# Small operands as weights in four groups of array columns: the heads' score products of a four-layer graph network

## The chip, the cores and the metric

The kernel runs on one core of a Trainium2 chip. The metric is the device time of one execution in microseconds (us), the median of several runs.

## What is computed

Four graph layers over 3327 nodes with 128 features each; after each layer comes x = layernorm(x + layer(x)). The adjacency matrix `adj` (3327 x 3327, float32) is the same in all. The change touches layer 4, whose attention part is, cut down:

```python
def _gat_head(h, node_adj, edge_adj, W, a):        # 3 heads, ALPHA = 0.2
    hW = h @ W
    hp = (node_adj > 0).astype(hW.dtype) @ hW
    hm = (node_adj < 0).astype(hW.dtype) @ hW
    e_plus = leaky_relu(concatenate([hp, hm], axis=1) @ a, ALPHA)[:, 0]
    e_minus = leaky_relu(concatenate([hm, hp], axis=1) @ a, ALPHA)[:, 0]
    att = where(edge_adj > 0, e_plus[None, :], NEG_INF)
    att = where(edge_adj < 0, e_minus[None, :], att)
    return softmax(att, axis=1) * edge_adj @ hW
...
node_support = node_adj_norm @ h                   # adj without its diagonal
edge_output = _gru_cell(node_support, h, edge_Wih, edge_Whh, edge_bih, edge_bhh)
edge_support = mean over the heads of _gat_head(h, node_adj_norm, edge_adj_norm, gat_W[i], gat_a[i])
node_output = _gru_cell(edge_support, h, node_Wih, ...)
return de[:, None] * edge_output + dn[:, None] * node_output
```

Since `(A > 0) @ (h @ W) @ a` is `(A > 0) @ (h @ (W a))`, the kernel needs only, for each node, six numbers `h @ (W a)` (two halves of `a` for three heads: the **column scores**), and the pattern sums of these. Of the sums, three a node are the heads' **raw scores**, from which e_plus follows.

## The kernel before, in words

Nodes are padded to 3328 and stand in 26 tiles of 128 (`TILES`); the columns of the adjacency in 7 blocks (`BLOCKS`, six of 512 and one of 256; `NB` = 7, `BT` = 4 tiles a block). SBUF tiles of note: `x` (nodes on partitions), `xT` (its transpose, features on partitions), `ring` (13 slots of 128 x 512 for pieces of `adj`), `pos8` (the pattern adj > 0 in fp8, in `arena`), `V` (in `shared`, the pattern sums), `es`/`unb` (scratch, in `es`), `hb`. `ps` is PSUM, 8 banks of 128 x 512 float32.

Layer 4's first half is one queue on TensorE, written out by hand:

- `dense4(b, between)` multiplies block b of adj with x: 26 products of 512 columns (L1169) into bank b % 2, each waiting for its slot of the ring; `between` names what is done behind which tile. SyncE refills a slot when its product has freed it (L493), so loads run 13 tiles ahead. GpSimd zeroes the diagonal piece of four tiles a block (`ring_cuts`, L639) before they are used (`cut_ring`).
- `turn` (L973) transposes x into xT, with ScalarE's `turn_copy` (L685) emptying banks 2 and 3.
- Column scores (L1178): for each of the 26 tiles, 128 columns of xT are the weights and the six columns of `v6` the moving operand; results go to bank 3. VectorE splits them into three bf16 parts in `gs` (L1744 to L1749, from PSUM directly).
- `edge_gates(g)` (L1149 to L1151) are the products of the gated cell for two tiles, four of them in blocks 1 and 2, whose element work VectorE (`edge_cell`, L1760 to L1781) and ScalarE (L808, L812) do.
- `pattern_sums` (L1190): V = gs-columns x pos8, on strips of 32 array columns, t % 4 choosing the strip; ScalarE copies each block of V out of PSUM (L826). SyncE writes V to DRAM once it is complete (`kept`, L507), between the ring's loads of tiles 12 and 13 of block 2.
- Raw scores (L1206): for each of 26 tiles, 128 columns of V are the weights and three columns of `selE` (0 and 1, adding up the 32-row strips) the moving operand; results go to bank 2. VectorE (L1818 on) takes leaky relu, the heads' maxima (`turn_maxima`, L1211), a rounded maximum spread to all partitions (`spread_maxima`, L1215), the range (`turn_range`, L1219), and the window weights `wh` (to L1862).
- `window_sums` (L1231) with `turn_sums` (L1239) stand behind block 3; the head loop (L1321) ends the first half's work.

The column scores stand between `turn` and block 1, the raw scores between the pattern sums and block 2:

```python
                pe.wait_ge(xT_done, 2 * NB)
                for t in range(TILES):
                    last = mm(ps[:, 3, 6 * t:6 * t + 6], lhsT=xT[:, t * P:(t + 1) * P],
                              rhs=v6[:].rearrange("p a k -> p (a k)"), start=True, stop=True)
```

Of the kernel before, what the change touches and what calls it, by code (L numbers as in the profile page):

```python
# [38 lines left out]
def program(nc, d, out):  # L39
    ctx = ExitStack()  # L40
    with ctx:
# [3 lines left out]
        def sem(name):  # L45
            return ctx.enter_context(nc.semaphore(name))
# [11 lines left out]
        def piece(space, at, width):  # L58
            return space[:, at:at + width]
# [39 lines left out]
        gscr = piece(bench, 0, 6 * TILES).rearrange("p (t r) -> p t r", r=6)  # L99
# [24 lines left out]
        v6 = sb("v6", [P, 2, HEADS])  # L124
# [94 lines left out]
        cols_done = sem("cols_done")  # L219

# [199 lines left out]
        def tiles_of(b):  # L420
            return range(b * BT, min((b + 1) * BT, TILES))

# [239 lines left out]
        def _(act):  # L662
# [156 lines left out]
            for b in range(NB):  # L819
                turn_copy(NB + b, b, 2 + b % 2)  # L820
            edge_cell(0)
            edge_cell(1)
            u3_copy(1)
            for b, (o_, w) in enumerate(BLOCKS):
                act.wait_ge(v_done, b + 1)
                A_(V[:, o_:o_ + w], ps[:, 2 + b % 2, 0:w], ACT.Copy).then_inc(v_out, 1)  # L826
            act.wait_ge(est, TT_READY)
# [117 lines left out]
        def _(pe):  # L945
# [146 lines left out]
            def after_layer2(negative):  # L1092
# [82 lines left out]
                turn(2 * TILES, NB, (2, 3))  # L1175
                pe.wait_ge(xT_done, 2 * NB)
                for t in range(TILES):
                    last = mm(ps[:, 3, 6 * t:6 * t + 6], lhsT=xT[:, t * P:(t + 1) * P],  # L1178
                              rhs=v6[:].rearrange("p a k -> p (a k)"), start=True, stop=True)
                last.then_inc(cols_done, 1)  # L1180
                dense4(1, {4: lambda: edge_gates(0), 14: lambda: edge_gates(1)})
# [22 lines left out]
                pe.wait_ge(v_out, NB)  # L1204
                for t in range(TILES):
                    last = mm(ps[:, 2, HEADS * t:HEADS * (t + 1)], lhsT=V[:, t * P:(t + 1) * P], rhs=selE[:, 0:HEADS], start=True, stop=True)  # L1206
                last.then_inc(raw_done, 1)
# [13 lines left out]
                dense4(2, {2: turn_maxima, 4: spread_maxima, 8: turn_range, 12: lambda: edge_gates(2), 20: lambda: edge_gates(3)})  # L1221
# [146 lines left out]
        def _(ve):  # L1368
# [23 lines left out]
            def late_steps():  # L1392
                ve.wait_ge(late_prod, 1)
                step(v.tensor_copy(v6[:], ps[:, 6, 0:2 * HEADS].rearrange("p (k a) -> p a k", a=2)))
                step(v.tensor_tensor(gru[:, 3], gru[:, 3], ps[:, 6, P:P + G3], ALU.subtract))
                check(steps[0], V6_READY)
                step(v.tensor_tensor(b2[:], b2_two[:, 0], b2_two[:, 1], ALU.add))
                check(steps[0], B2_READY)
                step(v.tensor_tensor(gb[:, :, 1:3].rearrange("p e a f -> p e (a f)"),
                                     gb[:, :, 1:3].rearrange("p e a f -> p e (a f)"), stage, ALU.add))  # L1400
                step(v.scalar_tensor_tensor(state_weights[:, 0:G3], state_weights[:, 0:G3], lone[:], gru[:, 3], ALU.mult, ALU.add))
                step(v.tensor_scalar(state_weights[:, G3:], state_weights[:, G3:], lone[:], None, ALU.mult))
                step(v.tensor_scalar(others[:], lone[:], -1.0, 1.0, ALU.mult, ALU.add))
                step(v.tensor_copy(ident16, ident[:]))
                check(steps[0], LATE_READY)

# [335 lines left out]
            g6 = ps[:, 3, 0:6 * TILES].rearrange("p (t r) -> p t r", r=6)  # L1742
# [75 lines left out]
            then(v.tensor_copy(raw, ps[:, 2, 0:Q78]))  # L1818
# [267 lines left out]
V6_READY = 35  # L2086
B2_READY = 36
LATE_READY = 41
GS_READY = 53
# [5 lines left out]
OUT_READY = 57  # L2095
# [48 lines left out]
```

## Time and profile before

| | us |
|---|---|
| three runs: median (lowest to highest) | 1450.9 (1450.29 to 1452.09) |
| profiled execution: span from first to last instruction (the one time it gives) | 1449.1 |
| its TensorE matmuls busy | 1339.7 (92%) |
| VectorE busy | 906.9 (63%) |
| ScalarE busy | 543.8 (38%) |
| GpSimd busy | 187.7 (13%) |
| mean granted TensorE clock | 0.966 of full |

The page of a profile is one execution. PE is TensorE's matmuls, PEld its weight loads, DVE VectorE, ACT ScalarE, POOL GpSimd, SPq the queue of SyncE's DMAs. The span leaves out what lies before the first and behind the last instruction: the runs' median is 1.8 above it. A float32 product stands in the trace as two matmul records, so "x52" at L1178 is 26 products. Layer 4's first half runs from 668 us to about 927 us.

### The profile page before, as it was taken

To read this page: it belongs to the slowest core of one execution; us is meant where nothing else is said; L and a number is where in the kernel's file an instruction comes from. 1 tells how busy PE (TensorE), PEld (TensorE's weight loads), DVE (VectorE), ACT (ScalarE), POOL (GpSimd) and SP (SyncE) were. 2 spreads that over 40 slices of the span, in tenths; PEclk is the share of its full clock that TensorE was granted. 3 is DMA by queue.
4 is the path that set the end of the run, shared out by engine and by line. 5 is a ranking of instruction groups with operands and counts; after the bars stand their busy time and mean duration, and the time that the engine had idled before them with its cause. 6 is when DMAs were issued, how large, how long until landed. Compare 5 with 4: busy or idle time off the path is not lost.

```text
span 1449.1 us, 11441 instructions
## 1 busy us (share of the span) xinstructions
PE 1339.7 (92%) x4198; PEld 675.7 (47%) x4198; DVE 906.9 (63%) x1187; ACT 543.8 (38%) x469; POOL 187.7 (13%) x211
## 2 busy tenths in 40 slices
PE   3888886899989999999999999999999999999993
PEld 1333334444444444455655454644445444544451
DVE  4787777888865000003125363599878987898576
ACT  4444444867630000000111001455564565555333
POOL 0000002000020000000000000124431244113111
PEclk9999997899999999999899999999999999999997
DMA  9999993000026767758447339698876888688301
GB/s 380 427 426 416 419 390 107 2 0 0 0 96 175 196 192 196 193 150 275 149 164 236 105 109 325 211 363 327 307 281 252 329 304 310 229 306 329 141 0 50
DMA packets 78002, 321.27 MB, mean 222 GB/s; under 512 B 8685, under 2 KB 20588, under 8 KB 61036
## 3 DMA queue, kind: packets, MB, share of 16 engines
q1 hardware_dynamic: 77931, 320.40, 61.9%
q8 instruction: 37, 0.61, 0.2%
q14 instruction: 34, 0.27, 0.1%
HBM read 316.94 MB, written 3.43 MB: 221 GB/s over the span
## 4 chain that ended last, share of the span: by engine, by line
PE 82%; DMA 10%; DVE 5%; ACT 1%; issue 1%; SPq 0%; POOL 0%; ACTq 0%; DVEq 0%; POOLq 0%
PE ps L1321 29%; PE ps L1132 10%; PE ps L1169 10%; PE ps L1066 10%; DMA ring<-in_adjR 9%; PE ps L991 6%; PE ps L1126 5%; PE ps L1231 2%; PE ps L1342 1%; PE ps L1303 1%; PE ps L1150 1%; PE ps L1343 1%; DMA ring<-in_adjB 1%; PE ps L1106 1%; PE ps L1151 1%; PE ps L1190 1%
## 5 line engine op out<-in xcount | busy, mean ns | idle before, releaser
L1321 PE MATMUL ps<-arena,x 128*128 128x512 f32 (+1 forms) x1092 | 438.9, 562 | 2.9 <-ACT shared L894 1.6
L1321 PEld LDWEIGHTS ps<-arena,x 128*128 128x128 f32 x1092 | 206.1, 190 | 231.4 <-issue 225.2
L887 ACT ACTIVATE arena<-arena,bench 128x3328 f32<-128x3328 bf16 x78 | 239.8, 3075 | 188.8 <-PE ps L1321 176.4
L991 PE MATMUL ps<-ring,bench 128*128 128x512 f32 (+1 forms) x364 | 171.9, 617 | 51.1 <-DMA ring<-in_adjR 48.9
L1982 DVE TENSOR_TENSOR arena<-arena,ring 128x3328 f32<-128x3328 f32 x51 | 184.9, 3625 | 27.3 <-ACT arena L887 26.8
L1132 PE MATMUL ps<-ring,x 128*128 128x512 f32 (+1 forms) x364 | 176.2, 566 | 0.0
L1169 PE MATMUL ps<-ring,x 128*128 128x512 f32 (+1 forms) x364 | 152.1, 573 | 1.0 <-DMA ring<-in_adjB 1.0
L991 PEld LDWEIGHTS ps<-ring,bench 128*128 128x128 f32 x364 | 70.8, 206 | 130.6 <-issue 97.1
L1691 DVE SCALAR_TENSOR_TENSOR bench<-b,cols,ps 128x128 f32<-128x128 f32 x26 | 7.3, 343 | 183.1 <-PE ps L1106 183.1
L651 POOL TENSOR_TENSOR ring<-ring,nid 128x128 f32<-128x128 f32 x51 | 86.0, 1686 | 205.2 <-DMA ring<-in_adjR 205.2
L1126 PE MATMUL ps<-arena,shared 128*128 128x512 fp8e4 (+1 forms) x364 | 103.6, 366 | 6.1 <-DVE shared L1496 6.1
L1982 DVE TENSOR_TENSOR arena<-arena 128x3328 f32<-128x3328 f32 x27 | 98.1, 3632 | 13.0 <-ACT arena L887 13.0
L1169 PEld LDWEIGHTS ps<-ring,x 128*128 128x128 f32 x364 | 69.9, 194 | 72.6 <-issue 67.8
L1066 PE MATMUL ps<-ring,x 128*128 128x512 f32 (+1 forms) x196 | 82.2, 576 | 6.0 <-DVE ring L1616 5.7
L795 ACT ACTIVATE ub<-ps 128x512 f32<-128x512 f32 (+1 forms) x7 | 4.0, 567 | 208.2 <-PE ps L1132 208.2
L1126 PEld LDWEIGHTS ps<-arena,shared 128*128 128x128 f16 x364 | 35.7, 98 | 96.7 <-issue 85.5
L1132 PEld LDWEIGHTS ps<-ring,x 128*128 128x128 f32 x364 | 67.7, 192 | 23.1 <-issue 0.5
L1975 DVE TENSOR_SCALAR arena<-arena,bench 128x3328 bf16<-128x3328 bf16 x52 | 62.2, 1195 | 0.0
L1066 PEld LDWEIGHTS ps<-ring,x 128*128 128x128 f32 x196 | 37.4, 194 | 50.2 <-issue 47.6
L651 POOL TENSOR_TENSOR arena<-arena,nid 128x128 f32<-128x128 f32 x27 | 46.0, 1707 | 105.7 <-DMA arena<-in_adjR 105.6
L1440 DVE TENSOR_SCALAR arena<-ring 128x3328 fp8e4<-128x3328 f32 x26 | 49.0, 1883 | 1.2 <-DMA ring<-in_adjR 1.2
L1760 DVE TENSOR_TENSOR es<-ps,gb 128x512 f32<-128x512 f32 x12 | 8.3, 691 | 61.7 <-PE ps L1151 61.7
(289 smaller groups left out, 1427.8 us busy)
## 6 DMA issues: line engine op xcount, KB each, us to landing
ring<-in_adjR SPq DMA_DIRECT2D x77, 1664.0 KB, 8.7
ring<-in_adjB SPq DMA_DIRECT2D x312, 256.0 KB, 3.1
arena<-in_adjR SPq DMA_DIRECT2D x27, 1664.0 KB, 8.4
shared<-in_adj SPq DMA_DIRECT2D x7, 1664.0 KB, 13.4
es<-in_adj SPq DMA_DIRECT2D x7, 1664.0 KB, 13.4
xT<-in_adj SPq DMA_DIRECT2D x6, 1664.0 KB, 13.0
y<-in_adj SPq DMA_DIRECT2D x6, 1664.0 KB, 13.4
ring<-in_adjB SPq DMA_DIRECT2D x52, 128.0 KB, 2.3
```

What stands on the lines that cost most here:

```text
L651: g_.tensor_tensor(cut, cut, nid[:], ALU.mult).then_inc(row_cut, 1)
L887: A_(E[n % 3], below[n % 3], ACT.Exp, bias=tt_[:, t * HEADS + k:t * HEADS + k + 1], scale=-WIN).then_inc(e_exp, 1)
L991: op = mm(ps[:, b, 0:w], lhsT=scaled[:, t % 4], rhs=turned_tile[t % 2][:, o_:o_ + w], start=(t == 0), stop=(t == TILES - 1))
L1066: op = mm(ps[:, b, 0:w], lhsT=x[:, t], rhs=EL[t % 4][:, o_:o_ + w], start=(t == 0), stop=(t == TILES - 1))
L1126: mm(ps[:, 2 + par, 0:w], lhsT=x16[:, t, k], rhs=pos8[:, t, o_:o_ + w], start=first and k == 0, stop=final and k == 1)
L1132: mm(ps[:, par, 0:w], lhsT=x[:, t], rhs=ring[:, t % CHUNKS, 0:w], start=first, stop=final).then_inc(ring_free, 1)
L1169: mm(ps[:, b % 2, 0:w], lhsT=x[:, t], rhs=ring[:, t % CHUNKS, 0:w], start=(t == 0), stop=(t == TILES - 1)).then_inc(ring_free, 1)
L1231: last = mm(ps[:, b % 2, 0:w], lhsT=wh[:, t], rhs=pos8[:, t, o_:o_ + w], start=(t == 0), stop=(t == TILES - 1))
L1321: last = mm(ps[:, b, 0:w], lhsT=x[:, t], rhs=E[n % 3][:, o_:o_ + w], start=(t == 0), stop=(t == TILES - 1))
L1440: v.tensor_scalar(pos8[:, t], turned_tile[t % 2], 0.0, None, ALU.is_gt, saturate=False).then_inc(pos_done, 1)
L1975: v.tensor_scalar(below[n % 3], tops[k], raw[:, t * HEADS + k:t * HEADS + k + 1], 0.0, ALU.add, ALU.max).then_inc(lowered, 1)
L1982: v.tensor_tensor(E[n % 3], E[n % 3], row_at(n), ALU.mult).then_inc(q_ready, 1)
```

## The change

Both score groups swap their operands. The small operand (`v6`, now 32 columns wide with zeroes, or `some`, a copy of selE's three columns, also padded to 32) becomes the weights and a whole block of xT or V, 512 columns, moves. Block b's product goes to the array columns 32 (b % 4) and the partitions of the same numbers, in bank 2 for blocks 0 to 3 and bank 3 for blocks 4 to 6: seven products in place of 26 (`strips`). The scores now stand with nodes along the free axis, so ScalarE copies both banks to SBUF (`rows_copy`, in the scratch `unb`), and eight transposes (`turn_strips`) put nodes back on partitions. VectorE gathers the scores from PSUM by `by_tile`, three copies a group. The transposes, and for the raw scores the strips too, stand between products of blocks 1 and 2. In block 2 the later steps move: maxima behind tile 6 (2), spread 8 (4), range 12 (8), gates 14 and 21 (12 and 20).

```diff
-        v6 = sb("v6", [P, 2, HEADS])
+        padded = hb[:, 1, 0:64]
+        v6 = padded[:, 0:32]
+        some = padded[:, 32:64]
+        scores = unb
...
+        def by_tile(bank, rows):
+            by = ps[:, bank, :].rearrange("p (s q r) -> p q s r", s=BT, q=4)
+            if bank == 2:
+                return [(slice(0, 4 * BT), by[:, :, :, 0:rows])]
+            return [(slice(4 * BT, 6 * BT), by[:, 0:2, :, 0:rows]), (slice(6 * BT, TILES), by[:, 2, 0:TILES - 6 * BT, 0:rows])]
...
+            def rows_copy(done, out_):
+                act.wait_ge(done, 1)
+                A_(scores[:, 0], ps[:, 2, :], ACT.Copy).then_inc(out_, 1)
+                A_(scores[0:96, 1], ps[0:96, 3, :], ACT.Copy).then_inc(out_, 1)
+
+            rows_copy(scored, scores_out)
             edge_cell(0)
...
                 A_(V[:, o_:o_ + w], ps[:, 2 + b % 2, 0:w], ACT.Copy).then_inc(v_out, 1)
+            rows_copy(picked, picked_out)
...
+                def strips(weights, rows, done):
+                    for b, (o_, w) in enumerate(BLOCKS):
+                        q = 32 * (b % 4)
+                        last = mm(ps[q:q + 32, 2 + b // 4, 0:w], lhsT=weights, rhs=rows[:, o_:o_ + w], start=True, stop=True)
+                    last.then_inc(done, 1)
+
+                def turn_strips(out_, done):
+                    pe.wait_ge(out_, 2)
+                    for h, k in ((0, P), (1, 96)):
+                        for s in range(BT):
+                            last = nc.tensor.transpose(ps[:, 2 + h, s * P:s * P + k], scores[0:k, h, s * P:(s + 1) * P], ident[0:k, 0:k])
+                    last.then_inc(done, 1)
+
                 pe.wait_ge(xT_done, 2 * NB)
-                for t in range(TILES):
-                    last = mm(ps[:, 3, 6 * t:6 * t + 6], lhsT=xT[:, t * P:(t + 1) * P],
-                              rhs=v6[:].rearrange("p a k -> p (a k)"), start=True, stop=True)
-                last.then_inc(cols_done, 1)
-                dense4(1, {4: lambda: edge_gates(0), 14: lambda: edge_gates(1)})
+                strips(v6, xT, scored)
+                dense4(1, {2: lambda: turn_strips(scores_out, cols_done), 4: lambda: edge_gates(0), 14: lambda: edge_gates(1)})
...
-                pe.wait_ge(v_out, NB)
-                for t in range(TILES):
-                    last = mm(ps[:, 2, HEADS * t:HEADS * (t + 1)], lhsT=V[:, t * P:(t + 1) * P], rhs=selE[:, 0:HEADS], start=True, stop=True)
-                last.then_inc(raw_done, 1)
+                def pick():
+                    pe.wait_ge(v_out, NB)
+                    strips(some, V, picked)
...
-                dense4(2, {2: turn_maxima, 4: spread_maxima, 8: turn_range, 12: lambda: edge_gates(2), 20: lambda: edge_gates(3)})
+                dense4(2, {1: pick, 3: lambda: turn_strips(picked_out, raw_done), 6: turn_maxima, 8: spread_maxima, 12: turn_range,
+                           14: lambda: edge_gates(2), 21: lambda: edge_gates(3)})
...
-                step(v.tensor_copy(v6[:], ps[:, 6, 0:2 * HEADS].rearrange("p (k a) -> p a k", a=2)))
+                step(v.memset(padded, 0.0))
+                v.tensor_copy(some[:, 0:HEADS], selE[:, 0:HEADS])
+                step(v.tensor_copy(v6[:, 0:2 * HEADS].rearrange("p (a k) -> p a k", a=2), ps[:, 6, 0:2 * HEADS].rearrange("p (k a) -> p a k", a=2)))
...
-            g6 = ps[:, 3, 0:6 * TILES].rearrange("p (t r) -> p t r", r=6)
+            for bank in (2, 3):
+                for ts, got in by_tile(bank, 6):
+                    of = g6[:, ts] if len(got.shape) == 3 else g6[:, ts].rearrange("p (q s) r -> p q s r", s=BT)
+                    op = v.tensor_copy(of, got)
+            step(op)
...
-            then(v.tensor_copy(raw, ps[:, 2, 0:Q78]))
+            for bank in (2, 3):
+                for ts, got in by_tile(bank, HEADS):
+                    of = raw[:, ts.start * HEADS:ts.stop * HEADS]
+                    op = v.tensor_copy(of.rearrange("p (t k) -> p t k", k=HEADS) if len(got.shape) == 3
+                                       else of.rearrange("p (q s k) -> p q s k", s=BT, k=HEADS), got)
+            then(op)
```

TensorE's queue from the column scores into block 1, before (the lines are the kernel's; a row is a run of equal instructions, output <- operands, shape of the output; `v` is v6):

```order
L1178 MATMUL ps<-v,xT 128x6 x26
L1169 MATMUL ps<-ring,x 128x512 x5
L1149 MATMUL ps<-gru,ub 128x128
L1150 MATMUL ps<-gru,xT 128x384
L1151 MATMUL ps<-gru,ub 128x256
```

and with the change, where line numbers have moved (L1199 the strips, L1206 the turns back, L1189 the dense products, L1169 to L1171 the gates; `hb` holds v6, `es` the copied rows):

```order
L1199 MATMUL ps<-xT,hb 32x512 x6
L1199 MATMUL ps<-xT,hb 32x256
L1189 MATMUL ps<-ring,x 128x512 x3
L1206 MATMUL ps<-ident,es 128x128 x4
L1206 MATMUL ps<-ident,es 128x96 x4
L1189 MATMUL ps<-ring,x 128x512 x2
L1169 MATMUL ps<-gru,ub 128x128
L1170 MATMUL ps<-gru,xT 128x384
L1171 MATMUL ps<-gru,ub 128x256
```

26 products before block 1 have become seven, and eight transposes stand behind block 1's third tile.

TensorE's queue from the raw scores through block 2's first steps, before:

```order
L1206 MATMUL ps<-selE,shared 128x3 x26
L1169 MATMUL ps<-ring,x 128x512 x3
L1211 MATMUL ps<-ident,mx 3x128
L1169 MATMUL ps<-ring,x 128x512 x2
L1215 MATMUL ps<-dm,ones 128x3
L1169 MATMUL ps<-ring,x 128x512 x4
L1219 MATMUL ps<-ident,rmax 1x128
```

and with the change:

```order
L1199 MATMUL ps<-shared,hb 32x512 x6
L1199 MATMUL ps<-shared,hb 32x256
L1189 MATMUL ps<-ring,x 128x512 x2
L1206 MATMUL ps<-ident,es 128x128 x4
L1206 MATMUL ps<-ident,es 128x96 x4
L1189 MATMUL ps<-ring,x 128x512 x3
L1240 MATMUL ps<-ident,mx 3x128
L1189 MATMUL ps<-ring,x 128x512 x2
L1244 MATMUL ps<-dm,ones 128x3
L1189 MATMUL ps<-ring,x 128x512 x4
L1248 MATMUL ps<-ident,rmax 1x128
L1189 MATMUL ps<-ring,x 128x512 x2
```

Block 2's first two tiles now follow the pattern sums directly; strips, two tiles, the turns back, and three more tiles come before the maxima's transpose (L1240), then spread (L1244) and range (L1248) at the old distances.

## Rows read from the trace of the kernel before

**Rows 1.** Page, part 4: the chain that ended last, by engine.

```profile
PE 82%; DMA 10%; DVE 5%; ACT 1%; issue 1%; SPq 0%; POOL 0%; ACTq 0%; DVEq 0%; POOLq 0%
```

**Rows 2.** Chain from 665 to 940 us: start us, us, what ran, matmul records.

```profile
668.07 22.33 PE ps L1169 x52
...
695.35 9.49 PE ps L1178 x52
704.84 5.81 PE ps L1169 x10
...
733.88 9.96 PE ps L1190 x175
...
743.86 0.39 ACT shared L826
...
744.29 7.42 PE ps L1206 x52
751.71 4.55 PE ps L1169 x6
...
821.62 0.44 PE ps L1239 x4
822.05 5.61 PE ps L1231 x26
```

**Rows 3.** Busy time by window: stretch, us, busy per engine (count), granted clock (PEclk).

```profile
core 0: us, PE busy (x) PEld busy (x) DVE busy (x) ACT busy (x) POOL busy (x), PEclk, DMA share, GB/s
...
690.40:695.30 4.90, 3.51 (x26) 2.50 (x24) 0.00 (x0) 4.13 (x8) 0.00 (x0) 1.00 0.54 184
695.30:697.30 2.00, 1.95 (x18) 1.95 (x18) 0.00 (x0) 1.28 (x1) 0.00 (x0) 1.00 0.00 0
697.30:704.80 7.50, 7.50 (x38) 7.50 (x37) 0.00 (x0) 0.00 (x0) 0.00 (x0) 0.50 0.01 2
704.80:707.60 2.80, 2.80 (x5) 1.25 (x5) 2.04 (x6) 0.00 (x0) 0.00 (x0) 0.51 0.00 0
...
744.20:748.50 4.30, 4.21 (x38) 4.21 (x38) 0.00 (x0) 0.04 (x1) 0.00 (x0) 1.00 0.82 346
748.50:751.70 3.20, 3.20 (x17) 3.20 (x16) 0.00 (x0) 0.00 (x0) 0.00 (x0) 0.51 0.18 73
751.70:755.20 3.50, 3.50 (x6) 1.43 (x6) 0.74 (x3) 0.00 (x0) 0.00 (x0) 0.50 0.07 12
```

**Rows 4.** Line L1190 alone: ns min/median/max of a record, shapes, counts.

```profile
L1190 PE MATMUL ps<-arena,gs x182: 272/379/393, 733.8 to 743.5; 128*32 128x512 fp8e4 x156, 128*32 128x256 fp8e4 x26
```

**Rows 5.** Timeline of ScalarE, 742 to 762 us: start, us, line, [idle before].

```profile
743.09 0.60 ACT L826 ACTIVATE shared<-ps 128x512 f32<-128x512 f32 x1 [0.91 <-PE ps L1190]
```

**Rows 6.** Timeline of VectorE, 690 to 850 us, same columns.

```profile
704.88 0.48 DVE L1744 CAST gs<-ps 128x156 bf16<-128x156 f32 x1 [33.22 <-PE ps L1178]
...
751.75 0.24 DVE L1818 COPY bench<-ps 128x78 f32<-128x78 f32 x1 [22.45 <-PE ps L1206]
...
752.30 0.26 DVE L1820 TENSOR_REDUCE mx<-bench 128x3 f32<-128x78 f32 x1
756.48 0.28 DVE L1823 TENSOR_REDUCE mq<-ps 3x1 f32<-3x128 f32 x1 [3.93 <-PE ps L1211]
...
757.32 0.22 DVE L1827 TENSOR_SCALAR dm<-ident,mq 3x3 f32<-3x3 f32 x1
...
762.25 0.28 DVE L1842 TENSOR_REDUCE row<-ps 1x1 f32<-1x128 f32 x1 [1.70 <-PE ps L1219]
...
771.44 0.20 DVE L1862 TENSOR_SCALAR bench<-bench 128x78 f32<-128x78 f32 x1
```

**Rows 7.** DMA issues, 735 to 765 us: count, KB each, us to landing.

```profile
ring<-in_adjB SPq DMA_DIRECT2D x12, 256.0 KB, 3.1
V_kept<-shared SPq DMA_DIRECT2D x1, 1664.0 KB, 6.1
```

**Rows 8.** Timeline of TensorE, 860 to 945 us, same columns.

```profile
927.08 5.75 PE L1321 MATMUL ps<-arena,x 128*128 128x512 f32 x14
```

More of the change, by code:

```diff
@@ L98, in program @@
         raw, e_, dd, idx, ctr, tt_, r1, r2, v_ = (piece(bench, k * Q78, Q78) for k in range(9))
-        gscr = piece(bench, 0, 6 * TILES).rearrange("p (t r) -> p t r", r=6)
+        gscr, g6 = (piece(bench, k * 6 * TILES, 6 * TILES).rearrange("p (t r) -> p t r", r=6) for k in range(2))
         hb = sb("hb", [P, 2, F])
@@ L219, in program @@
         cols_done = sem("cols_done")
+        scored = sem("scored")
+        scores_out = sem("scores_out")
+        picked = sem("picked")
+        picked_out = sem("picked_out")
         f1_done = sem("f1_done")
@@ L2085 @@
 XSB_READY = 27
[L2086 to L2089, printed above, removed]
+V6_READY = 36
+B2_READY = 37
+LATE_READY = 42
+GS_READY = 55
 MX_READY = 3
@@ L2094 @@
 WH_READY = 23
-OUT_READY = 57
+OUT_READY = 59
 DOWN = 2.718281828459045 ** -64
```

## The prediction, made before the changed kernel had run

> **What bounds the kernel now.** I read the chain that ended last first, then the chain inside layer 4's first half, then the granted clock along it, and last the timelines of the engines that TensorE hands over to. The page's chain is 82% TensorE [rows 1], so work taken off TensorE counts unless something else was about to end at the same time. In the stretch that the change touches the chain is all TensorE [rows 2]: block 0's 26 tiles (52 records, two passes each, since every float32 product here leaves two matmul records) take 22.33 us, that is 0.859 us a tile; then come the turns of x, the column scores at L1178 (9.49 us), block 1, the pattern sums at L1190 (9.96 us), a wait for ScalarE's last copy of V (from 733.88 + 9.96 = 743.84 to 744.29, 0.45 us), the raw scores at L1206 (7.42 us), and block 2.
>
> The reader is to see three things. First, the two score groups are bound by weights, not by columns: 26 products of 6 columns cost 0.365 us each and 26 of 3 columns 0.285 us each, with the weight loads busy for all of the stretch (1.95 of 2.00 us, 7.50 of 7.50) [rows 3]. Second, the clock: while x is turned it is granted in full, two microseconds into the column scores it falls to half (1.2 GHz instead of 2.4) and stays there until 707.6, well into block 1; in the raw scores it falls at 748.5 and is back only at 755.2 [rows 3]. So block 1's first 5 tiles took 5.81 us where 5 x 0.859 = 4.29 are usual, and block 2's first 3 took 4.55 instead of 2.58 [rows 2]. Third, nothing but the two groups' consumers hangs on them: VectorE waits 33 us for the column scores and 22 us for the raw ones [rows 6].
>
> **The change, part by part.** Removed from the chain: L1178 9.49, L1206 7.42, the 0.45 ahead of it (two tiles of block 2 now stand there instead, 1.7 us), and the half-clock tails 5.81 - 4.29 = 1.52 and 4.55 - 2.58 = 1.97. Sum 20.85 us. The tails go only if the clock holds, which is a rival below.
>
> Added, for each group: seven products with 32 columns of weights, six of 512 moving columns and one of 256. What such a product costs in float32 is not in the trace, so I bound it. One after the other they take as much as dense tiles, 6 x 0.859 + 0.43 = 5.58 us. Four at once, as the pattern sums do it, they take two rounds, 2 x 0.859 = 1.72. That strips on 32 columns do run side by side is shown: L1190's 182 products (156 of 512 columns, 26 of 256, so 169 full ones) last 9.96 us, 0.059 each [rows 2, 4], against 0.216 for a one-pass product on all columns (5.61 us for 26) [rows 2]. But there neighbours in the queue are always different strips. Here each product is two passes on the **same** strip, in order: the second pass of strip 0 waits for the first, and only strip 1's first pass can run beside it. Then a pass starts every 0.43 us and the group takes 6 x 0.43 + 0.43 = 3.0 us. I take 3.0, between the ends 1.7 and 5.6, since queues of matmuls start in order in every row I have.
>
> The Trainium skill (TensorEngine Tiling (Array Packing), Theoretical Speedup) gives up to four times for a dimension of 32 or less, and says nothing there of two passes. By it the group would take the 1.72 us of the last end and the sum below would be 2.6 us larger; that is the first rival.
>
> Around a group the array goes from all columns to strips and back. L1190 shows the most this can cost: 9.96 us against 169 x 0.216 / 4 = 9.13, so 0.83 with seven hand-overs to ScalarE in it. I take 0.3 a group, ends 0 and 0.8.
>
> The eight turns back: four turns take 0.44 us between products [rows 2], so eight take 0.88, and the four of 96 columns no more. Per group 3.0 + 0.3 + 0.88 = 4.2 us, both 8.4. **Sum: 20.85 - 8.4 = 12.45, say 12.5 us off TensorE's chain.**
>
> What stands beside other work, with its cover. ScalarE copies the two banks: 0.60 us each [rows 5], with hand-overs some 1.4 us from the last strip to the turns' start. The cover is three dense tiles (2.58 us) in block 1 and two (1.72 us) in block 2; the second has 0.3 us to spare, and without cover the cost is at most 1.4 us each. ScalarE is idle at both places. VectorE takes three small copies in place of one (0.24 us for the raw ones [rows 6], 0.5 more), three for the column scores where there were none (up to 0.48 each, 1.4 us), and a memset and a copy far earlier in layer 3. The column scores' chain, 704.88 to 707.1, is wanted only by L1190 a block later. The raw scores' chain: 752.56 - 751.75 = 0.8 us to the heads' maxima, now 1.3, behind three dense tiles (2.58). From the maxima to the spread two tiles, 1.72 us, against the five steps from 756.48 to 757.54, 1.06 us and a hand-over on either side [rows 6]; from there to the range four tiles as before, where VectorE even waited 1.70 us [rows 6]. The chain to the window weights ends 9.4 us behind the range turn (762.25 to 771.64) [rows 6]. Block 2's gates now come at 14 and 21 instead of 12 and 20, still behind it or level; the next taker, the window sums, is over 30 us away.
>
> SyncE and GpSimd: no DMA is moved in the order. The load of block 2's tile 13 stands behind the write of V, 6.1 us [rows 7], which waits for V's last copy. It used to run beside L1206; now it runs beside block 2's own tiles. The ring holds 13 tiles, 11 us of products, plus strips and turns, so tile 13's load has about 15 us for 6.1 + 3. After that the ring has to refill at the pace of the products: 26 loads of 256 KB in 22.33 us without a wait, as in block 0 [rows 2, 7]. I cost it at nothing; if the lead were gone it would be a few tenths a tile.
>
> Everything behind block 2 starts from TensorE's own progress (frees of the ring, window sums, head loads), so the 12.5 us should reach the end whole. Span 1449.1 - 12.5 = 1436.6; the runs' median 1450.9 lies 1.8 above the span, so the forecast is **1438.4 us**.
>
> **The rivals.** *Four at once.* For: L1190 does it. Against: two passes on one strip. Groups of 1.72 instead of 3.0: 1435.8 us.
>
> *One at a time.* If a two-pass product holds the whole array, or strips with different moving data can't overlap in this type: 5.58 a group, 5.2 us less gain, 1443.6 us. For it speaks only that no two-pass strip is in the trace.
>
> *The clock falls anyway.* Here a stretch of half clock lasts 10.3 and 6.7 us [rows 3], and costs half of that in work: 5.1 + 3.4 = 8.5 us, so 1446.9. For: x's turns come right before, with TensorE busy only 3.5 of 4.9 us [rows 3], and the strips are short. Against: the clock was 1.00 through the turns and fell only in the 6-column products [rows 3], and through L1190's strips the chain ran at full pace. The Trainium skill (TensorE: Matmul & The Clock Gate, Part 4: PE-mode transpose) says that turns don't count as activity, which would make this case likelier; the trace here disagrees as far as it goes, since five microseconds of turns left the clock at 1.00.
>
> *Slower.* The strips run one after the other **and** at half clock throughout, at L1178's place and at block 2's: 2 x 5.58 + 2 x 0.88 + 0.3 = 13.2 us a group, and the tails of 3.5 us stay. 26.4 + 3.5 against 20.9 is 9.0 us longer, 1459.9. It decides from 10.4 us a group; one of the two halves alone doesn't reach it.
>
> *It moves nothing.* The ring or VectorE gives the gain back (a wait in block 2 of the size of the gain), about 1450. The rows show leads of 15 us and over 30 us against it.
>
> **How the numbers follow.** Pairs 0.45, four at once 0.25, one at a time 0.16, clock falls 0.08, moves nothing 0.03, slower 0.03. The predicted time is that of pairs. The range goes from four at once with no cost of switching (1435.8 less 0.6, and a half more for a clock that shifts elsewhere) to one at a time with the dear switching (1443.6 + 1.0): 1434.6 to 1444.8. Left out are the clock case and the last two. A measurement of this kernel tells some 0.2%, 2.9 us, from no change. All cases but the last two are faster by more: 0.94; within 0.03; slower 0.03.
>
> **What would show it.** In the new profile the strips' line shows 14 records a group in about 3 us, their starts 0.43 us apart: 0.86 apart would be one at a time, groups of starts together four at once. The granted clock from 695 to 715 and around 745 reads 1.00, and block 1's first tiles take 0.86. TensorE waits for neither ScalarE's copies nor the ring in blocks 1 and 2. The head loop's first matmul starts about 12.5 us before 927.08 [rows 8]. A group above 5 us, a clock of 0.50 behind it, or a shift that shrinks before 927 would each prove a step wrong.

## The result

The changed kernel takes 1434.53 us (median of four runs, 1432.49 to 1435.09) against 1450.81 before (four runs too): ratio 0.9882, 95% interval 0.9866 to 0.9898, so 16 us or 1.2% faster. The forecast was 1438.4 with a range from 1434.6 to 1444.8. The direction held, the size didn't: the gain is 4 us larger, and the time lies just below the range, by 0.07 us, which is less than the runs differ among themselves.

The profiled execution's span is 1433.5 us instead of 1449.1. Its chain, in the page's part 4:

```profile
PE 83%; DMA 9%; DVE 5%; ACT 1%; issue 1%; SPq 0%; POOL 0%; ACTq 0%; DVEq 0%; POOLq 0%
```

And the chain through layer 4's first half (start us, us, what; the rows answer to [rows 2]):

```profile
668.57 22.33 PE ps L1189 x52
...
695.85 1.91 PE ps L1199 x12
697.76 2.77 PE ps L1189 x6
700.53 0.77 PE ps L1206 x8
701.30 1.75 PE ps L1189 x4
...
726.27 9.94 PE ps L1220 x176
736.21 1.91 PE ps L1189 x4
738.12 1.84 PE ps L1199 x12
739.96 1.91 PE ps L1189 x4
741.88 0.77 PE ps L1206 x8
742.64 2.60 PE ps L1189 x6
...
795.78 11.38 PE ps L1261 x52
```

Block 0 takes the same 22.33 us. The column scores' 9.49 us have become 1.91, the raw scores' 7.42 us 1.84, the turns back 0.77 each. Block 1's first three tiles take 2.77 us, where before its first five took 5.81. From block 0's first tile to the first window sum the stage takes 795.78 - 668.57 = 127.21 us; before it took 810.23 - 668.07 = 142.16 (its last row below, with the end of the next stretch). So 14.95 us went here, of 15.6 in the whole span.

```profile
810.23 11.38 PE ps L1231 x52
...
936.29 3.64 DVE arena L1982
```

The head loop's first matmul starts at 911.35 instead of 927.08 [rows 8], 15.7 us earlier. The granted clock is now full all through the stage (answering to [rows 3]; stretch, us, busy us and count per engine, granted clock, DMA share, GB/s):

```profile
690.90:695.80 4.90, 3.50 (x26) 2.50 (x24) 0.00 (x0) 4.14 (x8) 0.00 (x0) 1.00 0.46 153
695.80:697.80 2.00, 1.95 (x15) 0.52 (x16) 0.00 (x0) 0.00 (x0) 0.00 (x0) 1.00 0.00 0
697.80:703.00 5.20, 5.20 (x20) 2.76 (x21) 1.53 (x7) 2.36 (x3) 0.00 (x0) 1.00 0.55 150
...
738.10:740.00 1.90, 1.90 (x16) 0.46 (x16) 0.00 (x0) 0.00 (x0) 0.00 (x0) 1.00 0.88 364
740.00:745.30 5.30, 5.30 (x20) 2.75 (x21) 0.87 (x5) 1.08 (x2) 0.00 (x0) 1.00 0.66 231
```

The rest of the 15.6: from the window sums to the head loop's second row 124.79 us instead of 126.06, 1.27 less; the head of the program, up to block 0, 0.50 more; the head loop and all behind it 0.12 more. The 1.27 goes with the wait for a load of the ring in block 5, 1.01 us before and absent in this profile. It isn't something the change aims at. In the profiles below the wait is 2.0 us (e5), 1.2 (e2), 0.9 (e4), 0.7 (e3), 0.6 (e7), 0.5 (e8) and absent (e1, e6, e9, e10). The other 0.26 comes and goes with it: less their wait, all seven profiles that have it take 125.05 to 125.07 us for this stretch, while this profile, e1 and e9 take 124.79 to 124.88 (e6, without a wait that shows, takes 125.18).

How four strips share the array is seen best in the strips' own line, in steps of 0.05 us through the raw scores' group (busy us and records of TensorE's products, then of its weight loads):

```profile
738.05:738.10 0.05, 0.05 (x4) 0.05 (x8) 1.00 2.50 1065
738.30:738.35 0.05, 0.05 (x4) 0.00 (x0) 1.00 0.00 0
738.50:738.55 0.05, 0.05 (x8) 0.04 (x3) 1.00 1.94 799
738.75:738.80 0.05, 0.05 (x4) 0.00 (x0) 1.00 0.00 0
738.90:738.95 0.05, 0.05 (x7) 0.01 (x3) 1.00 0.00 0
739.35:739.40 0.05, 0.05 (x5) 0.00 (x0) 1.00 0.00 0
739.60:739.65 0.05, 0.05 (x2) 0.00 (x0) 1.00 2.51 1065
```

Four products start together at 738.05, and all eight weight loads of the four strips' first products, for both passes, are under way within those 0.05 us. Until 738.5 there are four records, then eight overlap for a moment (the second passes start, the ends of the first are modelled), four again, and at 738.9 the next round's first three, which are the passes of blocks 4 to 6. No pass of strip 1 waited for the second pass of strip 0.

### The profile page after: what moved, and what is told of

Its sections match the earlier page's. It is cut to its first block, busy times and chain, and to the rows that moved or that the text cites. A ratio compares the mean times of both kernels' runs of the same rounds, so it can differ in the third digit from the quotient of the medians.

```text
span 1433.5 us, 11332 instructions
## 1 busy us (share of the span) xinstructions
PE 1322.4 (92%) x4138; PEld 658.3 (46%) x4138; DVE 906.7 (63%) x1194; ACT 546.0 (38%) x473; POOL 189.3 (13%) x211
## 4 chain that ended last, share of the span: by engine, by line
PE 83%; DMA 9%; DVE 5%; ACT 1%; issue 1%; SPq 0%; POOL 0%; ACTq 0%; DVEq 0%; POOLq 0%
PE ps L1351 30%; PE ps L1152 10%; PE ps L1189 10%; PE ps L1086 10%; DMA ring<-in_adjR 8%; PE ps L1011 6%; PE ps L1146 5%; PE ps L1261 2%; PE ps L1372 1%; PE ps L1333 1%; PE ps L1170 1%; PE ps L1373 1%; PE ps L1126 1%; DMA y<-in_adj 1%; PE ps L1171 1%; PE ps L1220 1%
## 5 line engine op out<-in xcount | busy, mean ns | idle before, releaser
L1189 PE MATMUL ps<-ring,x 128*128 128x512 f32 (+1 forms) x364 | 149.2, 563 | 0.0
L1189 PEld LDWEIGHTS ps<-ring,x 128*128 128x128 f32 x364 | 68.3, 190 | 69.8 <-issue 67.4
L1657 DVE TENSOR_TENSOR ring<-ring,arena 128x3328 f32<-128x3328 f32 x13 | 46.8, 3617 | 0.0
```

The lines of the kernel that those rows point to most:

```text
L1189: mm(ps[:, b % 2, 0:w], lhsT=x[:, t], rhs=ring[:, t % CHUNKS, 0:w], start=(t == 0), stop=(t == TILES - 1)).then_inc(ring_free, 1)
L1657: v.tensor_tensor(EL[t % 4], EL[t % 4], pos8[:, t], ALU.mult).then_inc(q1, 1)
```

## The experiments

Since the head of the program alone moves by up to 6 us from one execution to the next (block 0's first tile starts between 666.4 and 672.3 us in the twelve profiles), single spans can't tell 2 us. I compare the stage from block 0's first tile to the first window sum, which is 142.16 us before and 127.21 changed (127.23 in a second profile, e9).

**e1: neighbours in the queue on the same strip.** Blocks 0 and 1 go to the same strip, in banks 2 and 3, blocks 2 and 3 to the next, and so on. ScalarE's copies keep their shape; VectorE's copies follow the new layout.

```diff
-                        q = 32 * (b % 4)
-                        last = mm(ps[q:q + 32, 2 + b // 4, 0:w], lhsT=weights, rhs=rows[:, o_:o_ + w], start=True, stop=True)
+                        q = 32 * (b // 2)
+                        last = mm(ps[q:q + 32, 2 + b % 2, 0:w], lhsT=weights, rhs=rows[:, o_:o_ + w], start=True, stop=True)
```

> The strips' products stand in the other order: blocks 0 and 1 are neighbours in the queue and go to the same strip of 32 array columns (one in bank 2, one in bank 3), blocks 2 and 3 to the next, and so on; the amount of work and all that follows is the same. In the changed kernel a group takes 1.84 us between the tiles around it. Theory A (each strip has its own order; a product that waits for its strip doesn't hold up those behind it for other strips): a group stays at 1.7 to 2.0 us, four matmul records start together at its beginning, and the kernel's time stays at that of the changed kernel within 1 us. Rival B (matmuls start in the order of the queue, and the changed kernel ran four at once only because neighbours were on different strips): strip 0's four passes run first and the next strip joins only at its last one, 4 to 4.5 us a group, some 5 us longer in all.

The chain of e1, same columns:

```profile
699.57 1.93 PE ps L1199 x11
701.51 2.77 PE ps L1189 x6
...
741.87 1.86 PE ps L1199 x11
```

and the strips' line at the start of its first group, as above for the changed kernel:

```profile
699.60:699.65 0.05, 0.05 (x4) 0.05 (x8) 1.00 0.00 0
```

1.93 and 1.86 us, and the stage 127.26: theory A. With two products a strip, what stands next to what in the queue doesn't matter: a product whose strip is busy doesn't hold up those behind it. Four records are under way 0.05 us into the group (a strip works on one at a time, as e7 shows below), so the fourth strip's product runs although six stand ahead of it, of which three, one a strip, still wait. That is the step of my prediction that fails (e1's time, 1438.9 us, is no counter-argument: block 0 starts at 672.29 here, 3.7 us late before anything changed has run).

**e7: one strip with more work than the others.**

```diff
-                    for b, (o_, w) in enumerate(BLOCKS):
+                    for b, (o_, w) in [(0, BLOCKS[0])] * 3 + list(enumerate(BLOCKS)):
```

> The changed kernel with block 0's product issued four times instead of once in each group (same weights, same result, three idle repeats), so that strip 0 has five products, and the other strips two, two and one. Theory A (each strip works off its own products; a group takes as long as its longest strip): 5 x 0.859 = 4.3 us a group, 2.4 more than the 1.84 to 1.91 now. Rival B (the work is shared over the strips, ten products in rounds of four): three rounds, 2.6 us a group. Rival C (in order of the queue, pairs): strip 0's four products first and the rest behind, 5.2 us or more.

```profile
697.78 4.48 PE ps L1199 x18
702.26 2.77 PE ps L1189 x6
...
742.63 4.41 PE ps L1199 x18
```

4.48 and 4.41 us a group, where five products of two passes one behind the other are 5 x 0.859 = 4.3. Rival B's 2.6 and rival C's 5.2 are both excluded. The stage is 132.36, 5.15 above the changed kernel. So a group's time here is that of its fullest strip: with the seven blocks spread over four strips, two products, 1.72, plus 0.12 to 0.19.

That time alone doesn't show that the strips are free of each other, and the weight loads of this group show that they are not quite (timeline of TensorE's weight loads in e7, 697 to 703 us, columns as in [rows 6]):

```profile
697.78 0.14 PEld L1199 LDWEIGHTS ps<-xT,hb 128*32 128x32 f32 x2 [0.71 <-ACT xT L698]
698.24 0.11 PEld L1199 LDWEIGHTS ps<-xT,hb 128*32 128x32 f32 x1 [0.32 <-issue]
...
699.10 0.11 PEld L1199 LDWEIGHTS ps<-xT,hb 128*32 128x32 f32 x1 [0.32 <-issue]
699.53 0.15 PEld L1199 LDWEIGHTS ps<-xT,hb 128*32 128x32 f32 x7 [0.32 <-issue]
```

For the first 1.7 us only strip 0 works, one pass after the other, and the other three strips stand empty although their products are in the queue; the second group does the same (742.60 to 744.30). They start when the third of the four products at the head of the queue starts and only the fourth still waits. So in these runs one waiting product a strip is passed over (e1 has one on each of three strips), and two on the same strip hold up all that stands behind them. It costs nothing here only because strip 0 is the fullest either way.

**e5 and e6: one group alone.** e5 swaps the column scores only, e6 the raw scores only; the other group's lines are those of the kernel before.

```diff
# e5
-            rows_copy(picked, picked_out)
...
-                def pick():
-                    pe.wait_ge(v_out, NB)
-                    strips(some, V, picked)
+                pe.wait_ge(v_out, NB)
+                for t in range(TILES):
+                    last = mm(ps[:, 2, HEADS * t:HEADS * (t + 1)], lhsT=V[:, t * P:(t + 1) * P], rhs=selE[:, 0:HEADS], start=True, stop=True)
+                last.then_inc(raw_done, 1)
# e6
-            rows_copy(scored, scores_out)
...
-                strips(v6, xT, scored)
-                dense4(1, {2: lambda: turn_strips(scores_out, cols_done), 4: lambda: edge_gates(0), 14: lambda: edge_gates(1)})
+                for t in range(TILES):
+                    last = mm(ps[:, 3, 6 * t:6 * t + 6], lhsT=xT[:, t * P:(t + 1) * P], rhs=v6[:, 0:6], start=True, stop=True)
+                last.then_inc(cols_done, 1)
+                dense4(1, {4: lambda: edge_gates(0), 14: lambda: edge_gates(1)})
```

> Only the column scores are swapped, the raw scores stand as in the kernel before. Measured from block 0's first tile to the first window sum, where the kernel before takes 142.16 us and the changed one 127.21. Theory (the two groups are independent terms, each with its clock tail): L1178's 9.49 and the tail of 1.52 go, 1.84 for the strips and 0.77 for the turns and about 0.2 around them come: 142.2 - 8.2 = 134.0 us. The granted clock is 1.00 from 690 to 735 and falls once, in the raw scores. Rival (the second group only keeps its clock because the first no longer lowers it): the raw scores' stretch shows no fall here, and this kernel takes under 133.

> Only the raw scores are swapped, the column scores stand as in the kernel before. Theory (independent terms): L1206's 7.42, the wait of 0.45 and the tail of 1.97 go, 1.84 + 0.77 and about 0.4 around them come: 142.2 - 6.8 = 135.4 us from block 0 to the window sums, with the clock at 0.50 once, in the column scores and in block 1's first tiles. Both parts together are then 15.0, the whole of the change. Rival: a part that only the two together give, seen as a sum of both savings below 13.

e6 takes 135.33 us, 6.8 less than before, as expected. e5 takes 135.68, 6.5 less instead of 8.2. Its chain shows why:

```profile
736.59 9.21 PE ps L1235 x52
745.80 4.39 PE ps L1188 x6
```

The raw scores, the same 26 products as before, take 9.21 us here instead of 7.42: the clock fell 2.3 us into them, at 738.9, not 4.2 us in as in [rows 3], and was back at 749.1:

```profile
738.50:739.00 0.50, 0.50 (x6) 0.50 (x6) 0.00 (x0) 0.00 (x0) 0.00 (x0) 0.88 0.91 373
```

Nothing in these lines changed, only when they ran. So the two savings add up to 13.3, and the missing 1.6 of 14.95 is the clock's: what a stretch of small products costs hangs on when the clock happens to fall in it. The rival of e5 (no fall, under 133) is wrong, and so is my figure, and with it the 15.0 that I expected of the two parts together; e6's rival, a sum below 13, isn't met either.

The same rows give the price of a small product at each clock. At full clock 38 records, 19 products, take 4.21 us [rows 3], 0.22 us each. Counted at that price at full clock and at twice that price at half clock, 26 of them come to 9.5, 7.3 and 9.2 us for the column scores before, the raw ones before and the raw ones in e5 (2.0, 4.2 and 2.3 us of them at full clock), against 9.49, 7.42 and 9.21 measured. The 0.365 and 0.285 us of the prediction are mixtures of the two.

**e2 and e8: the old products, but never alone.** No operands swapped. The 26 small products a group stand between dense tiles: in e2 two behind each of 13 tiles in blocks 1 and 2; in e8 block 2 has four behind each of its first seven, so that VectorE gets the raw scores earlier. The other steps of block 2 move back, and VectorE splits the column scores between the two gated cells of block 1.

```diff
+                def some_cols(n):
+                    for t in (2 * n, 2 * n + 1):
+                        last = mm(ps[:, 3, 6 * t:6 * t + 6], lhsT=xT[:, t * P:(t + 1) * P],
+                                  rhs=v6[:].rearrange("p a k -> p (a k)"), start=True, stop=True)
+                    if n == TILES // 2 - 1:
+                        last.then_inc(cols_done, 1)
...
+                steps2 = {t + 1: (lambda n=t: some_raw(n)) for t in range(13)}
+                steps2.update({15: turn_maxima, 17: spread_maxima, 21: turn_range, 23: lambda: edge_gates(2), 25: lambda: edge_gates(3)})
# e8
+                steps2 = {t + 1: (lambda n=t: some_raw(n)) for t in range(7)}
+                steps2.update({9: turn_maxima, 11: spread_maxima, 15: turn_range, 17: lambda: edge_gates(2), 23: lambda: edge_gates(3)})
```

> The kernel before, with its 26 small products a group unchanged (128 columns of weights, 6 or 3 moving columns), but spread: two of them behind each of 13 dense tiles in block 1 and in block 2, so that the engine never runs a stretch of small products alone. The maxima, the spread and the range come at tiles 15, 17 and 21, the gates of block 2 at 23 and 25. Theory (the clock falls because of the stretch of small products, and the two tails of 3.5 us are part of what the change gains): granted clock 1.00 from 668 us to the window sums, block 1's and 2's tiles at 0.86 each, and each small product 0.285 us or less, as at full clock before: 9.49 + 7.42 become 14.8 or less, tails and the wait of 0.45 gone, so 6 us faster than before, near 1444.8; up to 10 us faster if a part of the weight loads hides behind the dense passes (0.2 a product). Rival 1 (the clock falls on its own, after the turns): still 0.50 for some 7 to 10 us in each block, and at most 1 us faster. Rival 2 (the swap brings nothing of its own, keeping the groups apart does it all): as fast as the changed kernel, 1434.5.

> As e2, the old small products between dense tiles, but the raw ones four behind each of block 2's first seven tiles instead of two behind thirteen, with the maxima, spread and range at tiles 9, 11 and 15 and the gates at 17 and 23. In e2 the clock held, a small product cost 0.22 us (0.34 a pair and 0.10 on the tile behind it), and the gain was given back in block 3, where TensorE waited 5.4 us for ScalarE's copy because VectorE was late with the window weights. Theory: that chain is 5 to 6 us earlier and the wait goes; the clock stays at 1.00; the stage from block 0 to the window sums takes 142.2 - 9.4 = 132.8 us, 5.6 longer than with strips. Rival (four small products between tiles lower the clock, or the chain is still late): over 135.

The 0.285 us that e2's text gives as the price at full clock is such a mixture; the price was 0.22.

e2: ratio to before 0.9981 (0.9966 to 0.9995), the stage 140.65 us, only 1.5 less where 6 were expected. But the parts went as the theory says. Block 1's steps (one tile, two small products) and what came of it in block 3, in the chain:

```profile
698.21 0.34 PE ps L1179 x4
698.55 0.96 PE ps L1169 x2
...
742.53 0.34 PE ps L1217 x4
...
783.97 0.59 ACT ub L804
...
784.60 0.80 PE ps L1149 x2
```

and TensorE's waits from 665 to 930 us (engine, line, what for: us in total, times, longest):

```profile
PE ps L1149 <- ACT ub L804: 5.9, 2, 5.4
PE ps L1169 <- DMA ring<-in_adjB: 1.2, 1, 1.2
```

Two small products take 0.34 us and the tile behind them 0.10 more, so 0.22 each, the same as alone at full clock: standing between large products doesn't make a small one cheaper, it keeps the clock. The granted clock is 1.00 from 668 to 784 us. A group's small products cost 5.7 us, with no tail. What it gave was then lost in block 3: the raw scores were ready 13 tiles late, VectorE's chain to the window weights ended behind them, the gated cells queued up behind it, ScalarE's copy of block 2 stood behind the cells, and TensorE waited 5.4 us for it, during which the clock fell as well (0.61 and 0.54 from 784 to 788).

e8 takes that chain forward and confirms it (the chain of e8, from block 0 to the window sums):

```profile
668.35 22.33 PE ps L1169 x52
...
741.07 0.79 PE ps L1217 x8
741.86 0.96 PE ps L1169 x2
...
801.71 11.38 PE ps L1245 x52
```

Its results: ratio 0.9915 (0.9888 to 0.9943), the stage 133.36 us, 8.8 less than before, with the clock at 1.00 and no wait for ScalarE's copies in block 3. The expectation was 132.8. So of the change's 14.95 us, 8.8 can be had without swapping anything, by keeping the small products between large ones. That is the clock: before, 10.3 + 6.7 = 17.0 us ran at half clock [rows 3], and half of that is 8.5. The swap itself is worth the other 6.15: with all that it adds to the tiles around it a group costs 6.1 and 6.0 us in e8 and 2.9 and 3.0 in the changed kernel. e2's rival 1 (the clock falls on its own behind the turns) is out, and its rival 2 (the swap brings nothing of its own) too.

**e3: no tiles over ScalarE's copies.**

```diff
-                dense4(1, {2: lambda: turn_strips(scores_out, cols_done), 4: lambda: edge_gates(0), 14: lambda: edge_gates(1)})
+                turn_strips(scores_out, cols_done)
+                dense4(1, {4: lambda: edge_gates(0), 14: lambda: edge_gates(1)})
...
-                dense4(2, {1: pick, 3: lambda: turn_strips(picked_out, raw_done), 6: turn_maxima, 8: spread_maxima, 12: turn_range,
+                dense4(2, {1: lambda: (pick(), turn_strips(picked_out, raw_done)), 6: turn_maxima, 8: spread_maxima, 12: turn_range,
```

> The changed kernel with the turns back right behind the strips, no dense tile between them in either block. Theory (the tiles between cover ScalarE's two copies, 1.4 us a group): TensorE waits 1.2 to 1.5 us for ScalarE before each group's turns, the time is 2.4 to 3.0 us above the changed kernel, and the clock stays at 1.00. Rival (such a gap behind the short strips is enough to let the clock fall): 0.50 behind one of the groups, 4 us or more above the changed kernel.

```profile
PE ps L1206 <- ACT es L837: 2.4, 2, 1.2
```

1.2 us a group, the clock at 1.00, the stage 129.66: 2.45 more. The tiles between are worth slightly less than the 1.4 us a group that the prediction gave for a lost cover.

**e4 and e10: more waits of the same kind.** e4 puts the transposes of x between block 0's tiles. e10 does that and takes two more waits off: the first window sum no longer waits for block 3's copy, which is of another bank, and the last turns stand behind block 4's second tile. e9 is the changed kernel again, as their partner.

```diff
-                dense4(0, {})
-                turn(2 * TILES, NB, (2, 3))
+                def turn_block(b):
+                    pe.wait_ge(x_done, 2 * TILES + min(BT * (b + 1), TILES))
+                    if b >= 2:
+                        pe.wait_ge(xT_done, NB + b - 1)
+                    for q, t in enumerate(tiles_of(b)):
+                        last = nc.tensor.transpose(ps[:, 2 + b % 2, q * P:(q + 1) * P], x[:, t], ident[:])
+                    last.then_inc(turned, 1)
+
+                dense4(0, {min(BT * b + 3, TILES - 1): (lambda b=b: turn_block(b)) for b in range(NB)})
...
-            u3_copy(0)
             for b in range(NB):
                 turn_copy(NB + b, b, 2 + b % 2)
+            u3_copy(0)
# e10 besides
-                        pe.wait_ge(u3_out, SUMS + 1)
+                        pe.wait_ge(u3_out, SUMS + b)
...
-                turn_sums(NB - 1)
...
+                    if b == SUMS + 1:
+                        between[1] = lambda: turn_sums(NB - 1)
```

> The changed kernel with one thing more: the transposes of x stand between the tiles of block 0, four behind every fourth tile, and ScalarE copies them out ahead of block 0's own result. In the changed kernel they take 4.95 us behind block 0 (690.90 to 695.85), of which TensorE is busy 26 x 0.11 = 2.9 us and waits for ScalarE the rest. Theory (the chain is TensorE's own work here, and waits on it can be covered by dense tiles): 1.5 to 2.0 us faster than the changed kernel, block 0 with its turns 25.2 us long. Rival (something else is due at the same time, x's normalisation on VectorE or the ring): no gain, and a wait inside block 0.

> The changed kernel once more, as the partner of e10 in the same call, since the totals of different calls differ by 1 to 2 us through stages ahead of layer 4. Expected from block 0 to the window sums 127.2 us again, from the window sums' start to the head loop's second row (VectorE's product of 3.6 us) 124.8 to 126 according to whether block 5 waits a microsecond for the ring; total 1434 to 1437.

> e4 (the transposes of x between the tiles of block 0) and two more waits covered: the first window sum, which writes bank 0, waits for ScalarE's copy of block 2 instead of block 3's, and the last turns of the window sums stand behind block 4's second tile instead of ahead of its first. The stage from block 0 to the window sums took 125.58 in e4 and 127.21 in the changed kernel. Theory (each of these waits is on the one chain): the waits of 0.8 us ahead of the window sums and of 1.1 us ahead of the last turns go too, 1.6 + 0.8 + 1.1 = 3.5 us faster than e9. Rival (the ring takes some of it back, as the wait of a microsecond in block 5 comes and goes): 2 to 2.7 us.

e4: the stage takes 125.58 us, 1.63 less than the changed kernel. Block 0 with its turns, from 668.04 to the last turn copied, is 25.6 us long, and TensorE waits only for the last block's copy. Its total, 1433.38, can't be told from 1434.53.

e10: the stage takes 124.80, 2.4 less, and from the window sums to the head loop's second row 123.62 instead of 124.88, 1.3 less: 3.7 together, against 3.5 expected; the span is 1430.0 against 1433.5. The medians are 1432.23 (1430.65 to 1433.95) and 1434.65 (1432.37 to 1435.02), ratios to before 0.9877 (0.9859 to 0.9895) and 0.9887 (0.9870 to 0.9903). The waits that remain for TensorE there:

```profile
PE ps L1360 <- DVE arena L2032: 1.3, 2, 0.9
PE ps L1126 <- ACT es L809: 0.7, 1, 0.7
PE ps L1169 <- ACT ub L817: 0.5, 1, 0.5
PE ps L1206 <- ACT xT L698: 0.5, 1, 0.5
```

By its profile e10 is the fastest version of this study, 3.5 us ahead of the changed kernel and 2.4 ahead of e4; the totals of its runs and of the changed kernel's overlap, so by timing alone that isn't settled.

## Why the prediction was wrong

**The step that failed** is the price of a group of strips. I had bounds of 1.72 and 5.58 us and took 3.0, "since queues of matmuls start in order in every row I have": a pass would start every 0.43 us, and only a strip's second pass beside the next one's first. The groups took 1.91 and 1.84, with four passes, one on each strip, running at once. e1 shows that they do so with neighbours on the same strip too, and e7 that a group takes as long as its fullest strip. (e7 also shows where order does count: two waiting products on one strip held up the others for 1.7 us; no strip of the changed kernel has two waiting.) The evidence I leaned on could not carry this: rows of matmuls on all columns say nothing of four strips that can each take work. The row that could, L1190 with 0.059 us a product [rows 2, 4], pointed to four at once, and I set it aside because of the two passes. Two groups, 1.1 us each: 2.25 of the missing 3.9 us. The first rival had this case at 0.25 and 1435.8.

The account of the 3.9: the stage gained 14.95 instead of 12.45, so 2.5 (strips 2.25, turns 0.2); behind it came 1.27, below; 0.6 was lost elsewhere in the span. The last 0.7 is no work of TensorE: the forecast put 1.8 us between span and median, and here the median, 1434.53, lies only 1.0 above the profiled span, since the profiled execution, 1435.09, was the slowest of the four.

**Fill and switching**: 0.3 a group forecast. The tiles behind and ahead of strips and turns take 2.77 instead of 2.58 and 1.91 instead of 1.72, that is 0.19 at a place. Adding strips, turns and these, the first group costs 2.90 us and the second 3.0, 5.9 together, and 20.85 - 5.9 = 14.95 is the stage's gain. So the 0.3 was right in size, 0.2 and 0.4. The turns took 0.77, not 0.88.

**Removed**: 20.85 us was right for this profile, tails included. The clock held, as forecast, and e2 and e8 show what had lowered it: the stretches of small products, not the turns ahead of them, and spread out the same products leave it alone. That means 8.5 of the 20.85 us were the clock's, not only the 3.49 of the tails: I read 0.365 and 0.285 us as the price of weights, and at full clock it is 0.22. The Trainium skill's rule that turns don't count as activity (TensorE: Matmul & The Clock Gate, Part 4: PE-mode transpose) made the clock rival; here the clock stayed at 1.00 through five microseconds of turns with pauses, in both kernels. That doesn't settle whether turns count: the small products too ran for 2.0 to 4.2 us before the clock fell. And the tails are no fixed amount: e5's raw scores cost 9.21 us instead of 7.42 with the same code.

**Behind the stage**, 1.27 us more than the forecast's "whole": the ring's wait in block 5 wasn't there. I had assumed that everything behind block 2 would keep its distances, and it does not quite: that wait comes and goes. The bottom of the range, 1434.6, held four at once and free switching, but not this wait; with it the range had to reach to about 1433. (Its own terms give 1434.7 and 1444.6 for the two ends.) Whether the change makes the wait rarer, or its absence in both profiles of the changed kernel and in e1 is chance, these runs don't settle.

**Cover**: right. ScalarE's copies are hidden (e3: 1.2 us a group without), and VectorE's three copies cost less than the 1.4 and 0.7 us I allowed, 0.45 and 0.37; its chain to the window weights ended at 760.6, 35 us ahead of its taker (timeline of VectorE in the changed kernel, 695 to 764 us, columns as in [rows 6]):

```profile
701.34 0.45 DVE L1777 COPY bench<-ps 128x96 f32<-128x96 f32 x3 [29.18 <-PE ps L1206]
...
742.68 0.37 DVE L1857 COPY bench<-ps 128x48 f32<-128x48 f32 x3 [20.99 <-PE ps L1206]
...
760.41 0.20 DVE L1903 TENSOR_SCALAR bench<-bench 128x78 f32<-128x78 f32 x1
```

e2 shows the other side of that lead: 13 tiles of delay, and it is used up, not at the window sums, where I looked, but at ScalarE's copy of block 2, which stands in its queue behind the gated cells.

**The other rivals**: one at a time (1443.6), the clock (1446.9), slower (1459.9) and no shift (1450) are all out. The 10.4 us a group from which slower was to decide leaves the tails out; with them staying, as that rival has it, the kernels are level at (20.85 - 3.49) / 2 = 8.7. The Trainium skill (TensorEngine Tiling (Array Packing), Theoretical Speedup) was right with "up to four times": seven products of 5.58 us in a row took 1.84 to 1.93, three times as fast. Seven doesn't divide by four, so two rounds, 1.72 us, would be 3.2 times; the last 0.12 to 0.21 us no run explains.

## What to carry to other kernels

Where a product has few columns on one side, look at what its other operand costs as weights: 26 loads of 128 x 128 float32 for 6 columns each cost 9.5 us (5.7 at full clock), the same product with the small operand as weights on four strips 1.9. Even without a swap, don't let such products stand alone: here that gave 8.8 of the 14.95 us, since between large ones they, and the large ones behind them, kept the full clock. Before you take a mean time for the price of a product, look at the clock it ran at. Then deal the products evenly over the strips, with no long row of products for one strip, and put something large over the copy and the turn back; and when moving a step by some tiles, follow every engine's queue behind it, not only the final taker.

## What was not expected of the hardware

- Strips work side by side also in float32, where each product is two passes: four passes ran at once, one a strip, and all eight weight loads for the first four products were under way within 0.05 us. A group took 1.84 to 1.93 us with two products on the fullest strip (in the changed kernel, e1), 4.41 to 4.48 with five (e7), so 0.86 us for each further product.
- A waiting product was passed over by those for other strips when it was the only one waiting on its strip (e1); with two waiting on strip 0, the other three strips stood empty for 1.7 us (e7).
- In stretches of products with 3 or 6 moving columns the granted clock fell to 1.2 GHz though the weight loads were busy all the time: it fell 2.0 us into the column scores and 4.2 us into the raw ones before, 2.3 us into the raw ones in e5; 10.2 us of half clock there, 6.7 before.
- Two small products between dense tiles cost 0.34 us and 0.10 on the tile behind them; four cost 0.79 and 0.10 (e8), 0.22 each in both, and 0.22 each alone at full clock (19 in 4.21 us, before).
